# Shared-expert pieces inside the scans, and VectorE for the second normalise, in a fused MoE, Mamba and MoE kernel

## The reference

```python
x = x + 0.5 * ffn(layernorm(x))
x = x + ssm(layernorm(x))
x = x + 0.5 * ffn(layernorm(x))
# ffn: 8 experts, top 1: xs = x * sigmoid(max logit); silu(xs @ gate[e]) * (xs @ up[e]) @ down[e]
#      + shared expert: silu(x @ sh_gate) * (x @ sh_up) @ sh_down     (256 x 256 each)
# ssm: x_proj = x @ W_x.T -> dt_x (64), B (16), C (16); dt = softplus(dt_x @ W_dt.T + b_dt)
#      h = exp(dt * A) * h + dt * B * x;  y = sum over 16 states of h * C;  y + x * D
```

## Time and profile before

| | us |
|---|---|
| median of 3 runs (lowest, highest) | 547.25 (546.84, 548.16) |
| the profiled execution | 548.89 |
| its span | 547.2 |
| PE, DVE, ACT, POOL busy | 442.1, 342.6, 261.0, 277.4 |
| mean granted clock of TensorE | 0.921 |
| transition, 134 to 183 | 49.0 |
| four scans, 183.0 to 385.9 | 202.9 |
| routing and shared expert, 385.9 to 453.6 | 67.7 |

### The profile page before, as it was taken

One profiled execution on the slowest core, in us unless ns is written; L12 is line 12 of the kernel. 1 busy time (PEld: TensorE's weight loads), 2 busy tenths in 40 slices (PEclk: granted clock), 3 DMA queues, 4 the chain that ended last, 5 costly groups with the idle time before them and its releaser, 6 DMA issues.

```text
span 547.2 us, 7087 instructions
## 1 busy us (share of the span) xinstructions
PE 442.1 (81%) x2236; PEld 308.7 (56%) x2236; DVE 342.6 (63%) x557; ACT 261.0 (48%) x499; POOL 277.4 (51%) x213
## 2 busy tenths in 40 slices
PE   1988899998777675796888688699789937999991
PEld 1855455554434465775775677689546523555550
DVE  5357244333665989998999899969757321333430
ACT  1200233331063899699899989767011001333330
POOL 6003266664120476688997989799200003466632
PEclk9869999999897999799799889879979985999997
DMA  8942022210410122131232133223041113132300
GB/s 291 383 123 65 21 77 62 67 47 20 153 60 0 42 77 78 59 108 49 91 100 94 44 101 100 83 62 104 1 136 58 54 63 82 57 93 84 112 30 8
DMA packets 33331, 45.69 MB, mean 84 GB/s; under 512 B 5258, under 2 KB 22478, under 8 KB 33296
## 3 DMA queue, kind: packets, MB, share of 16 engines
q1 hardware_dynamic: 28144, 34.70, 19.9%
q0 software_dynamic: 5152, 10.54, 6.6%
HBM read 37.33 MB, written 12.48 MB: 91 GB/s over the span
## 4 chain that ended last, share of the span: by engine, by line
PE 55%; DVE 23%; issue 9%; POOL 7%; ACT 3%; DMA 1%; DVEq 0%; POOLq 0%
PE bank L656 17%; DVE hs L1057 12%; PE bank L630 11%; PE bank L684 7%; PE bank L615 6%; POOL gs L378 3%; PE bank L770 3%; PE bank L585 2%; PE bank L753 2%; DVE stats L861 2%; DVE dbx_t L1041 2%; PE bank L672 2%; PE bank L667 2%; POOL xn_no L339 2%; PE bank L570 1%
## 5 line engine op out<-in xcount | busy, mean ns | idle before, releaser
L378 POOL TENSOR_TENSOR gs<-hs,c_sb 128x1024 f32<-128x1024 f32 x62 | 147.2, 2389 | 57.1 <-DVE hs L1057 50.6
L1057 DVE TENSOR_TENSOR_SCAN hs<-da,bank 128x1024 f32<-128x1024 f32 x64 | 145.1, 2277 | 4.7 <-PE bank L753 4.5
L753 PE MATMUL bank<-ident,dbx_t 128*128 128x128 f32 x512 | 74.0, 292 | 35.5 <-DVE hs L1057 32.4
L347 POOL DMA_INDIRECT da<-rows,row_token x46 | 47.3, 1029 | 102.2 <-DMA rows<-x_sb 55.9
L656 PE MATMUL bank<-w_gu,tt 128*128 x184 | 94.6, 638 | 3.9 <-ACT tt L434 3.9
L476 ACT ACTIVATE da<-dt_sb,a_neg 128x511 f32<-128x511 f32 x128 | 84.9, 712 | 13.8 <-DVE hs L1057 13.7
L753 PEld LDWEIGHTS bank<-ident,dbx_t 128*128 128x128 f32 x512 | 61.1, 150 | 49.3 <-DVE hs L1057 43.4
L490 ACT ACTIVATE dbx_t<-dtx_t,h_sb 128x256 f32<-128x256 f32 x194 | 83.7, 495 | 4.7 <-DVE dtx_t L1026 3.4
L967 DVE SCALAR_TENSOR_TENSOR q_sb<-th,bank 128x256 f32<-128x256 f32 x46 | 19.4, 421 | 103.4 <-ACT th L429 103.4
L770 PE MATMUL bank<-ident,gs 128*128 128x128 f32 x496 | 71.5, 292 | 8.2 <-POOL gs L378 8.0
L429 ACT ACTIVATE th<-bank,da 128x256 f32<-128x256 f32 x46 | 21.8, 474 | 102.8 <-PE bank L656 102.8
(11 more groups left out here) (118 smaller groups left out, 506.3 us busy)
## 6 DMA issues: line engine op xcount, KB each, us to landing
c_sb<-c_dram SPq DMA_DIRECT2D x64, 256.0 KB, 3.1
rows<-xn_no SPq DMA_DIRECT2D x8, 516.0 KB, 6.1
x_sb<-in_x SPq DMA_DIRECT2D x4, 512.0 KB, 6.4
w_gu<-in_gate_w SPq DMA_DIRECT2D x2, 1024.0 KB, 10.1
w_gu<-in_up_w SPq DMA_DIRECT2D x2, 1024.0 KB, 11.2
w_dn<-in_down_w SPq DMA_DIRECT2D x2, 1024.0 KB, 10.5
xn_no<-token_out SPq DMA_DIRECT2D x4, 512.0 KB, 6.3
rows<-x_sb SPq DMA_DIRECT2D x4, 512.0 KB, 3.5
```

Of the source, the lines that this page charges most:

```text
L347: nc.gpsimd.indirect_dma_start(out=xr[:, u, 0:WIDE[r]], out_offset=None, in_=rows[r], in_offset=bass.IndirectOffsetOnAxis(ap=row_token[:, ...
L378: nc.gpsimd.tensor_tensor(gs[:, s % 2], hs[:, s % RING], c_sb[:, s % RING].unsqueeze(1).to_broadcast([P, KC, L]), ALU.mult).then_inc(sc_g, 1)
L753: mm = nc.tensor.transpose(DBX[s % 2][:, k, i * P:(i + 1) * P], dbx_t[:, s % TURNS, i, k * P:(k + 1) * P], ident[:])
L1057: nc.vector.tensor_tensor_scan(hs[:, s % RING].rearrange(flat), da[:, s % RING].rearrange(flat), DBX[s % 2][:, :, :].rearrange(flat), 0.0, ...
```

## The change

In the second ffn the shared expert of batches 0, 1 and 2 moves into scans 1, 2 and 3 as quarters: a quarter is one half of the hidden values for 256 tokens. TensorE computes it in slots 11 to 14 (8 records of 128x256 into bank T), ScalarE's tanh follows in slots 12 to 15, VectorE's two multiplications behind scan instructions 12 to 15. The down products of batches 0 and 1 go to slots 2 and 3 of scans 2 and 3, their results to VectorE's slots 3 and 4, and their rows are written by SyncE in slot 10; the down product of batch 2 goes behind the last scan. There only batch 3 has gate/up products left, both behind `count`. In the first ffn the down product and results of batch 3 move from the transition into slots 2 to 4 of scan 0; its second gate/up product gets banks of its own, and the order of the transition changes on all engines. VectorE normalises in slot 8 of every scan; GpSimd doesn't any more. Projection steps, combine, skip, transposes, copies and router products get other slots, `BY_DVE` other shares (its sums go from 17, 15, 15, 15 tiles to 13, 10, 10, 13), and SyncE no longer waits for the last rows written.

```diff
-    BY_DVE = (((2, 2, 2, 1, 1, 2, 2, 2, 0, 0, 0, 1, 0, 1, 0, 1),) + ((1, 1, 2, 1, 1, 2, 2, 2, 0, 0, 0, 1, 0, 1, 0, 1),) * 2
-              + ((1, 1, 2, 1, 1, 1, 1, 1, 0, 1, 1, 1, 1, 0, 1, 1),))
-    ROUTES = (5, 10)
+    BY_DVE = ((2, 2, 1, 1, 1, 2, 1, 0, 0, 0, 1, 1, 1, 1, 0, 0), (1, 1, 1, 1, 0, 1, 1, 0, 0, 0, 1, 1, 1, 1, 0, 0),
+              (1, 1, 1, 1, 0, 1, 1, 0, 0, 0, 1, 1, 1, 1, 0, 0), (1, 1, 1, 1, 1, 1, 1, 0, 1, 0, 1, 1, 1, 1, 1, 0))
+    ROUTES = (4, 8, 13)
...
+        sg_th = th[:].rearrange("p u f -> p (u f)")[:, 0:L // 2]
+        sg_h = y_sb[:].rearrange("p a d -> p (a d)").rearrange("p (k t) -> p k t", k=KC)
...
-            return (H[0], H[1]) if fo == 0 or (r, b) == (0, BATCH - 1) else (T, Y)
+            return (H[0], H[1]) if fo == 0 else (YS[0], YS[1]) if (r, b) == (0, 3) else (T, Y)
+
+        def shared_no(r, b, fo):
+
+            return 2 * b + fo if r == 0 else 8 + fo
+
+        def by_quarters(r, b):
+
+            return r == 1 and b < 3
+
+        def hidden_rows(r, b):
+
+            return sg_h if by_quarters(r, b) or (r, b) == (0, 3) else sh_h[:, b % 2]
+
+        def shared_out(r, q):
+
+            return T if (r, q // 2) in ((0, 3), (1, 0), (1, 1)) else YS[q % 2]
...
+                if s % N == 10 and s >= 2 * N:
+                    rest_rows(s // N - 2)
             xn_rows(1)
-            for b in range(BATCH):
+            for b in range(2, BATCH):
                 rest_rows(b)
-            for u in range(4):
-                sp.wait_ge(ff_out[u], 16 * uses(u) * RUNS)
...
-                    if n == 3:
-                        if b == 0:
-                            rstd_of(1, BATCH - 1)
-                        else:
-                            rstd_of(2, b - 1)
-                            normalise(2, b - 1)
+                    if b == 0 and n == 6:
+                        rstd_of(1, BATCH - 1)
+                    if b > 0 and n == 3:
+                        rstd_of(2, b - 1)
...
+            def quarter_tanh(g):
+                act.wait_ge(sg_gu, g + 1)
+                if g == 0:
+                    act.wait_ge(pj_bt, BATCH - 1)
+                    act.wait_ge(c_rows, 16 * (BATCH - 1))
+                elif g % 4 == 0:
+                    act.wait_ge(pj_bt, min(g // 4 + BATCH - 1, BATCH))
+                    act.wait_ge(c_rows, 16 * min(g // 4 + BATCH - 1, BATCH))
+                if g > 0:
+                    act.wait_ge(sg_hidden, g)
+                nc.scalar.activation(sg_th, T[:, 0:L // 2], ACT.Tanh, scale=0.5).then_inc(sg_tanh, 1)
...
-                    if n in (13, 14):
-                        ln_copy(*((1, 6 + n - 13) if b == 0 else (2, 2 * (b - 1) + n - 13)))
+                    if n in (10, 11):
+                        ln_copy(*((1, 6 + n - 10) if b == 0 else (2, 2 * (b - 1) + n - 10)))
+                    if b > 0 and n >= 12:
+                        quarter_tanh(4 * (b - 1) + n - 12)
...
-            shared_tanh(0, 3, 0)
+            project_ln(0)
             ln_copies(1, 1)
-            project_ln(0)
-            shared_tanh(0, 3, 1)
+            for fo in range(KC):
+                shared_tanh(0, 3, fo)
...
+                pe.wait_ge(sh_x, (0, GT // 2 + 6)[r])
...
+                    dst = shared_out(r, q)
+                    if dst is T:
+                        pe.wait_ge(sh_x, n)
+                        pe.wait_ge(pj_max, (4, 8, 8)[(b + 1) % 4] if r == 1 or b == 3 else 0)
+                    elif q >= 2:
+                        pe.wait_ge(sh_x, n - 1)
...
+            def shared_quarter(g):
+                b, fo, h = g // 4, g % 2, g // 2 % 2
+                pe.wait_ge(ln_xnT, GT + 2 * b + 2)
+                if g > 0:
+                    pe.wait_ge(sg_hidden, g)
+                lo = b * L + h * L // 2
+                for w, half in ((0, T[:, 0:L // 2]), (F, T[:, L // 2:])):
+                    for k in range(KC):
+                        last = nc.tensor.matmul(half, w_gu[:, k, SHARED, w + fo * P:w + (fo + 1) * P],
+                                                xnT[:, k, lo:lo + L // 2], start=(k == 0), stop=(k == KC - 1))
+                last.then_inc(sg_gu, 1)
...
+                    if n in (2, 3) and b != 1:
+                        shared_down(*((0, 3), None, (1, 0), (1, 1))[b], (n - 2,))
+                    if n == 4:
                         skip(b)
-                    if more and n in (8, 10):
-                        turn_dt(b + 1, (n - 8) // 2)
-                    if n in (12, 13):
-                        ln_transposes(*((1, 6 + n - 12) if b == 0 else (2, 2 * (b - 1) + n - 12)))
+                    if more and n in (6, 8):
+                        turn_dt(b + 1, (n - 6) // 2)
+                    if n in (9, 10):
+                        ln_transposes(*((1, 6 + n - 9) if b == 0 else (2, 2 * (b - 1) + n - 9)))
+                    if b > 0 and 11 <= n < 15:
+                        shared_quarter(4 * (b - 1) + n - 11)
...
+            project_bt(0)
             shared_gate_up(0, 3, 0)
             ln_batch(1, 1)
-            project_bt(0)
             shared_gate_up(0, 3, 1)
             ln_batch(1, 2)
-            shared_down(0, 3)
...
-            route(1, 2)
-            shared_gate_up(1, 0, 0)
+            shared_down(1, 2)
             ln_batch(2, BATCH - 1)
             route(1, BATCH - 1)
-            shared(1, BATCH)
+            count(1)
+            for fo in range(KC):
+                shared_gate_up(1, 3, fo)
+            sequence(1)
+            shared_down(1, 3)
...
-                shared_hidden(r, 0, 0)
+                shared_hidden(r, (0, 3)[r], 0)
...
+            def shared_quarter(g):
+                b, fo, h = g // 4, g % 2, g // 2 % 2
+                dve.wait_ge(sg_tanh, g + 1)
+                nc.vector.scalar_tensor_tensor(out=sg_th, in0=sg_th, scalar=1.0, in1=T[:, 0:L // 2],
+                                               op0=ALU.add, op1=ALU.mult).then_inc(sg_mul, 1)
+                dve.wait_ge(sg_mul, g + 1)
+                nc.vector.tensor_tensor(sg_h[:, fo, h * L // 2:(h + 1) * L // 2], sg_th, T[:, L // 2:], ALU.mult).then_inc(sg_hidden, 1)
...
-                    if b == 0 and n == 1:
-                        combine(BATCH - 1)
-                    if b == 0 and n == 2:
-                        dve.wait_ge(back_x, BATCH)
-                        stats_of(1, BATCH - 1)
-                    if b == 0 and n == 9:
-                        normalise(1, BATCH - 1)
                     if b > 0 and n == 1:
                         add_y(b - 1)
                     if b > 0 and n == 2:
                         dve.wait_ge(sc_x, KC * b)
                         stats_of(2, b - 1)
+                    if n in (3, 4) and b != 1:
+                        shared_result(*((0, 3), None, (1, 0), (1, 1))[b], (n - 3,))
+                    if b == 0 and n == 5:
+                        combine(BATCH - 1)
+                    if b == 0 and n == 6:
+                        dve.wait_ge(back_x, BATCH)
+                        stats_of(1, BATCH - 1)
+                    if n == 8:
+                        normalise(*((1, BATCH - 1) if b == 0 else (2, b - 1)))
                     if more and n == 4:
                         project_bt(b + 1)
-                    if more and n in (5, 7):
-                        project_w(b + 1, (n - 5) // 2)
-                    if more and n in (6, 8):
-                        project_dt(b + 1, (n - 6) // 2)
-                    if more and n in (10, 12):
-                        project_dtx(b + 1, (n - 10) // 2)
+                    if more and n in (4, 5):
+                        if n == 5:
+                            project_dt(b + 1, 0)
+                        project_w(b + 1, n - 4)
+                    if more and n == 6:
+                        project_dt(b + 1, 1)
+                    if more and n in (7, 9):
+                        project_dtx(b + 1, (n - 7) // 2)
+                    if b > 0 and n >= 12:
+                        shared_quarter(4 * (b - 1) + n - 12)
...
-            shared_result(0, 2)
+            combine(1)
             normalise(1, 0)
-            combine(1)
             dve.wait_ge(back_x, 2)
             stats_of(1, 1)
+            shared_result(0, 2)
+            normalise(1, 1)
             combine(2)
-            normalise(1, 1)
             dve.wait_ge(back_x, 3)
             stats_of(1, 2)
             project_bt(0)
             for k in range(KC):
                 project_w(0, k)
-            shared_hidden(0, 3, 0)
             normalise(1, 2)
             for k in range(KC):
                 project_dt(0, k)
-            shared_hidden(0, 3, 1)
+            shared_hidden(0, 3, 0)
             for h in range(2):
                 project_dtx(0, h)
-            shared_result(0, 3)
             for s in range(2):
                 outer(s)
+            shared_hidden(0, 3, 1)
...
+            shared_result(1, 2)
             route(1)
-            shared(1, BATCH)
+            row_ids(1)
+            shared_result(1, 3)
```

(9 more changed lines are left out.)

103 lines of the change are left out of this document (47 added, 56 removed).

## The result

The changed kernel takes 555.84 us (median of four runs, 555.15 to 561.74); the kernel before took 547.7 us in its four (546.84 to 548.49). The ratio is 1.0153, with a 95% interval of 1.0111 to 1.0195: slower by 1.5%, 10.5 us above the forecast of 545.3 and 3.3 us above the upper end of its range. The profiled execution took 556.34 us for a span of 554.6, against 548.89 and 547.2: 7.4 us more in span.

A forecast was written before the change was run, and what follows sets the result against it. VectorE was taken to bound the scans and TensorE the stage behind them. Terms of -10.8, +10.1, +17.4, +2.0 and -20.6 summed to -1.9 us, which put the 547.25 us median at 545.3, range 536 to 552.5.

The forecast's parts named there:

- Part 1: Transition before scan 0: work leaves the chain, first scan at 172.2 instead of 183.01 us; -10.8 us.
- Part 2: VectorE's own work in the scans: normalise, quarters and shared results added, fewer outer products; +10.1 us.
- The rival in which VectorE keeps the port: Normalise in the scans: its four instructions take 1.3 us, three scans save 2.0 each; 539.3 us, chance 0.08.
- Part 3: New waits on VectorE in the scans, found by walking each engine's order; +17.4 us.
- (a): Scan 0, slot 3: VectorE waits for the down half, which needs bank T from ScalarE's second relu; +4.7 us.
- (c): Scan 3: +4.6 us at the quarters, +1.35 because routing and skip products share slot 4 with a down half.
- (b): Slots 12 to 15, scans 1 and 2: tanh of quarter 0 late behind ScalarE's decays and tiles; +3.35 us each.
- Part 4: TensorE's clock falling behind the slot 8 stall in scans 1 to 3: a third of 6.1 us, +2.0 us.
- Part 5: Behind the last scan: TensorE products leave, but the score waits behind a shared hidden half; -20.6 us.
- The rival of the low clock: Slot 8 stalls cost +6.1 us and the stage behind the scans gives -18.7; 551.3 us, chance 0.30.
- fewer waits form: Scans: half of the 17.4 us of new VectorE waits is hidden, clock costs nothing; 534.6 us, chance 0.20.
- the tail does not pay: Behind the last scan: gather waits for late row writes, only 15 us are won; 551 us, chance 0.06.

The follow-up runs named there:

- experiment 10: Changed kernel without quarters, with GpSimd normalising in scans 1 to 3 and VectorE's old outer product shares: 541.76 us, ratio 0.9899 to the kernel before.
- experiment 2: Changed kernel, but in scans 1 and 2 VectorE normalises behind the projection steps of slot 5, with GpSimd idle: 550.29 us, ratio 1.0021 to the kernel before.
- experiment 1: Changed kernel, but GpSimd normalises behind slot 3 of scans 1 to 3, as before: 547.17 us, ratio 0.9985 to the kernel before.
- Experiment 4: Changed kernel, but without quarters: the second shared expert stays behind the scans for all batches: 555.78 us, ratio 1.0123 to the kernel before.
- experiment 7: Changed kernel with GpSimd normalising, routing chain ahead of the shared hidden halves, and VectorE's old outer product shares: 536.43 us, ratio 0.9784 to the kernel before.
- experiment 8: Changed kernel with GpSimd normalising, routing chain ahead of shared hidden halves, and ScalarE's tanh ahead of decays in slots 12 to 15: 540.43 us, ratio 0.9873.
- experiment 9: Changed kernel with 24 unread TensorE transposes added beside the normalise in slot 8 of scan 3: 557.34 us, ratio 1.0133 to the kernel before.
- experiment 3: Changed kernel, but behind the last scan the routing chain stands ahead of both shared hidden halves of batch 3: 548.33 us, ratio 0.9972 to the kernel before.

## Why the prediction was wrong

**What bounds the kernel:** right, VectorE in the scans, TensorE behind them.

**Part 1:** right. First scan at 172.21 for 172.2, dtx at 168.03 for 168.2; experiment 10 shows the same 10.8 us by themselves.

**Part 2:** right in its prices. Three of the four normalise groups take 3.41 to 3.42 us; the fourth, in scan 3, takes 4.16, 0.75 more than forecast. Its sum for scan 3 is too low by itself: 3.33, 3.2 and 1.2 less 0.3 and less all of the 4.7 are 2.7, not 2.1. And the 1.3 us that it takes off for fewer outer products leave out that ScalarE has to make them, which comes back in part 3. The rival in which VectorE keeps the port did not happen, and experiment 2 shows that it is the GpSimd product that makes the difference. The Trainium skill's page "Perfetto Trace Analysis" (Optimizing Scalar/DVE Operations), which warns that moving an operation between these two engines may not help, has the result on its side: experiment 1 is 8.7 us faster (555.84 to 547.17) with the operation on GpSimd, where it was.

**Part 3** is the step that failed, in its term for scan 1. (a) is right: 4.16 us in slot 3, scan 0 57.64 for 57.6. (c) misses the 0.75 us ahead of scan instruction 7 in scan 3; its waits in slot 4 (0.68) and behind the router product (2.14) are there. (b) is right for scan 2 (60.57 for 59.6) and wrong for scan 1 (64.54 for 58.0). I walked slots 12 to 15 only, and took the moved projection steps as work that costs the same elsewhere. Slots 1, 4, 5 and 7 hold 4.35 us of waits that the walk put at nothing: 1.98 on ScalarE's exponent and logarithm (slots 4 and 5), 1.11 on TensorE's transposes of dt (slot 7), 1.26 on its addition (slot 1). Experiment 4 shows that they do not come from the quarters. Experiments 7 and 10 show that the packed slots alone don't make those of slots 4 and 5 and that the new shares of outer products bring them (that the new shares alone would not either is an estimate, under experiment 7); slot 7 goes with TensorE's level. The mechanism of (b) had the right size at the full clock, 2.03 us in slot 12 for 2.0, but not the right engine: experiment 8 shows that the tanh's place does not matter.

**Part 4** was sized too low. "I take a third" of 6.1 us was a choice without a row behind it: one spell behind the normalise costs 1.5 us in scan 3 (experiment 9), 1.7 in scan 1 and 1.2 of wait in scan 2 (two executions of the same code each). The forecast had worked out 1.85 for scans 1 and 2 and 2.4 for scan 3 and then took a third of the sum; where the level fell, about two thirds or more of these came. The 1.1 us in slot 7 of scan 1 are from a spell where the forecast had none. In the kernel after these are 1.5, 1.7 and 1.1, 4.3 us instead of 2.0; scan 2 stayed at 1.00 behind its normalise.

**Part 5:** right to 1.4 us, -19.2 for -20.6 between bounds of -18.7 and -22.2. The gate/up and down products that one bound had at 1.2 GHz ran partly there (8.74 and 5.30 us). The chain is as walked, and experiment 3 confirms the hidden half as its cause: 6.7 us.

Of the 9.5 us between forecast and result the waits of scan 1 in slots 1, 4 and 5 are 3.2, the clock 2.3 in the scans (4.3 less the 2.0 forecast) and 1.4 behind them, scan 3 1.5 (0.75 in its normalise, 0.75 ahead of scan instruction 7), and scan 2 1.0. That is 9.4, and the 1.4 behind the scans are put down to the clock by their sizes alone; by scan these leave scan 1 0.4 short and scan 3 0.4 over. The rival of the low clock had the right sign and the right places, but its 551.3 us is still 4.5 short of the result, because it kept part 3 as walked. The rivals in which fewer waits form and in which the tail does not pay did not happen.

What stays open: why the level fell behind the normalise in three of four scans and not in the fourth. The writes of rows moved into the scans, which the forecast put at nothing, were not tried apart. The time of slot 1 in scan 1 (1.26 us here, 0.51 in the execution of experiment 9) differs between executions of the same code and wasn't followed up.

## What to carry to other kernels

A change made of several parts is to be measured in parts: here the transition is worth 1.0% by itself, two small orders (which engine normalises, and the routing chain behind a hidden half that it does not need) cost 18 us together, and with both put right the change is 1.8% faster than before (ratio 0.982, 0.9789 to 0.9851) instead of 1.5% slower. When steps are packed closer together, or work is handed from one engine to another, note for each result when it is ready and when it is wanted: here there were 6.0 us between the two, the packing took 3.6, the handing over 3.2, and the rest of the wait is another 0.7 by which the result came later. Walk every slot in this way, not only those with new work. A stretch in which VectorE does not run a scan instruction left TensorE idle for 3.45 to 4.68 us here, so count what the clock then costs too. Work that is moved off a stage only pays once the chain that it used to hide has been shortened too.

## What the runs showed of the hardware

Four VectorE instructions of 128x256 with scalar operands take 1.37 us with GpSimd idle and 3.41 to 3.42 us when a GpSimd product of two inputs starts 0.16 us behind them. One by one, in scan 1, they take 0.39, 2.47, 0.40 and 0.40 us: the second ends just behind GpSimd's product. In scan 3 the same group took 4.16: there GpSimd was in the middle of three products without a gap (7.07 us from 378.61), and the first instruction took 1.15 us as well. The product itself took 2.45 us beside the group and 2.37 alone. ScalarE loads a table for 1.28 us ahead of the logarithm and again behind it, in the kernel before as in the one after: it is no part of the difference, but the list of prices in the prediction doesn't have these 2.6 us. After 3.45 and 3.46 us of idle time in the same place TensorE's granted clock was 0.50 in one execution and 1.00 in another, and the scan around it took 64.54 and 61.29 us. Of these 3.25 us 1.70 are in the waits that follow the clock (slots 11 and 12), 0.3% of the kernel's time. The four runs of the changed kernel spread over 6.6 us, and the longest, 561.74 us, had the lower mean granted clock, 0.904 against 0.925 in the profiled one.
